# One decoder layer on one core: another order in the attention cycles, the output product from rounded parts, and weight rests on GpSimd

## The chip, the cores and the metric
One core of a Trainium2 chip. The metric is device time in microseconds (us), one execution of the whole kernel; the median of several runs is given. Engines are named PE (TensorE), DVE (VectorE), ACT (ScalarE), POOL (GpSimd) and SP (SyncE, which issues most DMAs).

## The reference
The input is x, 8 sequences of 128 rows of 512 features, with a context of the same size. Three blocks follow each other, each with a residual sum and a LayerNorm after it. Cut to what matters:

```python
# block 1: polynomial unit and gated unit, both on x
approx = (x @ up_w.T) @ local_out.T + sum over 6 orders (d**m/m! * (x @ up_w.T)) @ fuse[m].T
block1 = approx + (silu(x @ g1.T) * (x @ u1.T)) @ d1.T
# block 2: cross attention, 32 heads of 128, no score scaling
q, k, v = rmsnorm(x) @ w_q.T, ctx @ w_k.T, ctx @ w_v.T
score = q @ k.T + position_bias        # -inf where the mask is False
block2 = x + (softmax(score) @ v) @ w_out.T
# block 3: gated unit with weights of -1, 0 and 1
block3 = ((silu((x @ Wg.T) * ag) * ((x @ Wu.T) * au)) @ Wd.T) * ad
```

The mask lets a row attend only to keys in the last 32 positions of a sequence.

## The kernel before
Batch elements go in two halves of four (512 tokens each). PE multiplies float32 data in two ways. An exact product takes plain float32 operands. A product "from rounded parts" splits both operands into a part rounded to fp32r on ACT (`*_hi`) and the rest `whole - hi` on DVE (`low`, L1288, `*_lo`), and adds hi*hi, hi*lo and lo*hi (`passes`, L543).

The attention stage is `attention(few)`. A mask with keys only in the last FEW = 32 positions takes the branch `few=True`, and that one runs here. It walks n from -7 to 64 over HN = 64 pairs of head and half. `shared(n)` is true for n 0 to 15 and 32 to 47: such a cycle makes keys and values of a head for both halves at once (256 columns, from rounded parts) and keeps the other half's piece (`kept_k`, `kept_v`). In n 16 to 31 and 48 to 63, which the code calls `late`, the kept pieces are used, and `keys` and `values` only raise their semaphores. Keys run LEAD_K = 7 ahead, queries LEAD_T = 6 ahead.

What PE does in a sharing cycle n is written out by hand, in this order: `queries(n+6)` into bank 0, `turn(n-1)` (transpose of the probabilities, bank 3), `weigh(n-2)` (output product, one tile of 32 rows per batch element, into the four acc banks), `keys(n+7)` (bank 1), `values(n)` (bank 3), `outer(n-1)` (values times output weights, bank 1), and in two cycles of four a half of `group_scores` (bank 2). In a late cycle: queries, keys if n+7 is sharing, turn, weigh, outer, values, scores. ACT copies every bank out to SBUF, in an order of its own: in a sharing cycle `copy_queries`, `copy_turned`, `split_k(n+8)`, `copy_keys`, `split_v(n+1)`, `copy_values`, `copy_outer`, `exponentials(n+1)`. DVE does `find_max`, `divide`, `add_mask`, `rest_k` and `rest_v`. Each engine works in the order of its program.

These waits stand around the change. `outer(n-1)` waits for the copy of `keys(n+7)`, since both use bank 1:

```python
pe.wait_ge(v_ok, n + 1)
pe.wait_ge(k_ok, min(n + LEAD_K + 2, HN))
pe.wait_ge(kept_k_ok, shared_count(min(n + LEAD_K + 1, HN - 1)))
```

`copy_keys` and `copy_values` of a sharing cycle are two ACT instructions each: the kept 128x128 piece (L1150, L1183), then 128x512 (L1153, L1186). The last block starts after the loop: `features` transposes its input into bank 0 in n = 62 and 63, `gate` and `up` of its first tile follow at n = 64.

POOL normalises rows (L480, L485) and takes a maximum over partitions (L509); it has nothing to do in most of the attention stage.

## Time and profile before

| | us |
|---|---|
| median of 3 runs | 755.46 (755.07 to 755.62) |
| the profiled execution | 753.72 |
| its span in the trace | 751.9 |
| PE busy | 716.2 |
| DVE busy | 522.2 |
| ACT busy | 408.6 |
| POOL busy | 94.8 |

The kernel has three stages in the trace: block 1 up to about 222 us, attention up to about 613 us, the last block to the end. A PE instruction's record is longer than the distance to the next one, because matmuls overlap; what a step costs PE is the distance from its first start to the next step's first start.

### The profile page before, as it was taken

Reading aid. Unit: us, or ns where it says so; the run is one execution under the profiler, and the core shown is the slowest. Engines: PE = TensorE matmul, PEld = TensorE weight load, DVE = VectorE, ACT = ScalarE, POOL = GpSimd, SP = SyncE. Lnnn points to the kernel's source line nnn. Section 1 sums busy time; section 2 is a strip of 40 time slices with the busy share of each in tenths; the row PEclk is TensorE's granted clock in tenths of the full one; section 3 lists DMA queues with packets and bytes.
Section 4 is the critical chain, followed back from the end, with each engine's and each line's share of the span. In section 5 each row is a group of like instructions: output and inputs, shape, how many; then the busy total and the mean of one; then the engine's idle time right before and its main releaser. Section 6 shows DMA issues by size and latency. Waiting matters only on the chain.

```text
span 751.9 us, 12237 instructions
## 1 busy us (share of the span) xinstructions
PE 716.2 (95%) x4082; PEld 555.7 (74%) x4082; DVE 522.2 (69%) x848; ACT 408.6 (54%) x747; POOL 94.8 (13%) x88
## 2 busy tenths in 40 slices
PE   8999999999999999999999999999999779998993
PEld 6788888888878878776667787877656257886882
DVE  6555687588664875686876678667897828669565
ACT  6333323432355676776776666666676644454552
POOL 2000000074003600000000000000050004105403
PEclk9999999999999999999999999999999999999997
DMA  8455532545556765677997776668785513442631
GB/s 307 152 206 206 179 119 70 163 168 187 183 208 199 251 195 181 216 258 233 306 316 236 240 238 190 192 215 267 263 297 180 169 44 117 135 151 98 204 122 56
DMA packets 70681, 145.10 MB, mean 193 GB/s; under 512 B 7920, under 2 KB 8192, under 8 KB 69984
## 3 DMA queue, kind: packets, MB, share of 16 engines
q1 hardware_dynamic: 69200, 137.26, 55.7%
q0 software_dynamic: 1200, 6.70, 2.3%
q8 instruction: 34, 0.56, 0.3%
q10 hardware_dynamic: 224, 0.39, 0.2%
q14 instruction: 23, 0.19, 0.1%
HBM read 142.23 MB, written 2.10 MB: 192 GB/s over the span
## 4 chain that ended last, share of the span: by engine, by line
PE 86%; DVE 5%; issue 3%; DMA 2%; ACT 2%; POOL 1%; SPq 0%; ACTq 0%; DVEq 0%; POOLq 0%
PE bank L543 38%; PE acc L543 16%; PE acc L846 8%; PE bank L751 7%; PE bank L824 7%; PE bank L716 7%; PE bank L778 1%; PE bank L729 1%; DMA b_raw<-b 1%; DMA a_raw<-a 1%; PE bank L575 1%; DVE tile_lo L1288 1%; ACT v_sb L1186 1%; DVE a_lo L1288 1%; DMA wq<-wqn 1%
## 5 line engine op out<-in xcount | busy, mean ns | idle before, releaser
L543 PE MATMUL bank<-feat_hi,a_hi 128*128 128x512 f32 x348 | 137.7, 396 | 2.2 <-ACT u_sb L1193 0.8
L543 PE MATMUL bank<-feat_lo,a_hi 128*128 128x512 f32 x348 | 136.5, 392 | 2.1 <-issue 2.1
L1288 DVE TENSOR_TENSOR a_lo<-a_raw,a_hi 128x1024 fp32r<-128x1024 f32 (+3 forms) x47 | 56.8, 1208 | 94.5 <-ACT a_hi L1000 86.9
L543 PE MATMUL acc<-b_hi,tile_hi 128*128 128x512 f32 x224 | 87.8, 392 | 4.9 <-DVE tile_lo L1288 3.0
L543 PE MATMUL acc<-b_hi,tile_lo 128*128 128x512 f32 x224 | 87.3, 390 | 0.0
L543 PEld LDWEIGHTS bank<-feat_hi,a_hi 128*128 128x128 f32 x348 | 65.9, 189 | 22.6 <-issue 4.0
L543 PEld LDWEIGHTS bank<-feat_lo,a_hi 128*128 128x128 f32 x348 | 65.9, 189 | 13.5
L846 PE MATMUL acc<-u_sb,prob_t 32*128 32x512 f32 x512 | 73.0, 640 | 0.0
L543 PE MATMUL bank<-feat_hi,a_lo 128*128 128x512 f32 x180 | 70.1, 389 | 0.0
L1017 ACT ACTIVATE tile_hi<-pair 128x512 fp32r<-128x512 f32 x54 | 33.9, 628 | 66.3 <-DVE pair L1350 37.4
L751 PEld LDWEIGHTS bank<-t_ring,xn 128*128 128x128 f32 x512 | 62.1, 192 | 8.5 <-issue 7.2
L445 POOL TENSOR_SCALAR scale<-moments 128x4 f32<-128x4 f32 (+1 forms) x9 | 2.6, 287 | 515.1 <-DVEq L1420 514.8
L1558 DVE TENSOR_REDUCE row_sum<-prob 128x4 f32<-128x512 f32 x64 | 43.7, 683 | 31.9 <-ACT prob L1174 30.5
L1160 ACT ACTIVATE t_ring<-bank 128x512 f32<-128x512 f32 x64 | 38.2, 597 | 46.3 <-PE bank L716 46.0
L751 PE MATMUL bank<-t_ring,xn 128*128 128x128 f32 x512 | 62.3, 275 | 0.0
L1193 ACT ACTIVATE u_sb<-bank 128x512 f32<-128x512 f32 x64 | 38.2, 598 | 28.4 <-PE bank L824 25.8
L543 PEld LDWEIGHTS acc<-b_hi,tile_hi 128*128 128x128 f32 x224 | 42.0, 188 | 15.6 <-DVE b_lo L1288 4.2
L543 PE MATMUL acc<-b_lo,tile_hi 128*128 128x512 f32 x136 | 52.9, 389 | 0.0
L1288 DVE TENSOR_TENSOR b_lo<-b_raw,b_hi 128x512 fp32r<-128x512 f32 x56 | 40.0, 715 | 14.9 <-ACT b_hi L1007 14.6
L1007 ACT ACTIVATE b_hi<-b_raw 128x512 fp32r<-128x512 f32 x56 | 34.8, 623 | 26.8 <-PE acc L543 21.6
L1026 ACT ACTIVATE gated<-bank 128x512 f32<-128x512 f32 x20 | 12.0, 598 | 67.8 <-PE bank L543 67.8
L543 PEld LDWEIGHTS acc<-b_hi,tile_lo 128*128 128x128 f32 x224 | 42.1, 188 | 8.6
(152 smaller groups left out, 1555.8 us busy)
## 6 DMA issues: line engine op xcount, KB each, us to landing
wqi<-ax SPq DMA_DIRECT2D x64, 256.0 KB, 3.3
wq<-wqn SPq DMA_DIRECT2D x64, 256.0 KB, 3.7
wv<-wvh SPq DMA_DIRECT2D x64, 256.0 KB, 4.0
wo<-bx SPq DMA_DIRECT2D x64, 256.0 KB, 4.0
a_raw<-w SPq DMA_DIRECT2D x22, 512.0 KB, 4.1
wk<-ax SPq DMA_DIRECT2D x43, 256.0 KB, 3.8
a_raw<-a SPq DMA_DIRECT2D x21, 512.0 KB, 5.4
b_raw<-b SPq DMA_DIRECT2D x34, 256.0 KB, 2.7
```

The lines of the kernel that those rows point to most:

```text
L543: mm = pe.matmul(out_ap, w, x, start=start and k == 0, stop=stop and k == len(products) - 1, skip_group_check=True)
L716: mm = pe.matmul(bank[0][:, c * P:(c + 1) * P], wq[par][:, c * P:(c + 1) * P], few_keys, start=True, stop=True)
L751: mm = pe.matmul(bank[2][:, b * P:(b + 1) * P].rearrange("p (k h) -> p h k", h=GH), xn[half][:, c, b * SEQ:(b + 1) * SEQ], t_ring[g % 2][: ...
L824: mm = pe.matmul(bank[1][:], few_values, wo[slot][:], start=True, stop=True)
L846: mm = pe.matmul(acc[b][:], prob_t[par][rows, 0:P], u_sb[par][rows, :], start=begins, stop=ends, skip_group_check=True)
L1007: act.activation(b_hi[par][:], b_raw[par][:], ACT.Copy).then_inc(b_hi_ok, 1)
L1017: act.activation(tile_hi[par][:], src, ACT.Copy).then_inc(tile_hi_ok, 1)
L1026: act.activation(gated[:], bank[0][:], ACT.Silu).then_inc(silu_ok, 1)
L1160: act.activation(t_ring[n // GH % 2][:, n % GH].rearrange("p c b k -> p (c b k)"), bank[0][:], ACT.Copy).then_inc(t_ok, 1)
L1193: act.activation(u_sb[n % 2][:], bank[1][:], ACT.Copy).then_inc(u_ok, 1)
L1288: return dve.tensor_tensor(out_ap, whole, high, ALU.subtract)
L1558: dve.tensor_reduce(row_sum[:], prob[n % 2][:], AX_X, ALU.add).then_inc(sum_ok, 1)
```

## The change
In sharing cycles PE's order becomes queries, `values(n)`, `weigh(n-2)`, `turn(n-1)`, `keys(n+7)`, `outer(n-1)`, scores. `turn(n-1)` now waits for the copy of `values(n)`, which has bank 3 before it. `weigh` of a sharing head becomes 12 matmuls of fp32r parts in place of 4 float32 ones: the rounded parts `p_hi` and `u_hi` come from ACT, the rests `p_lo` (128x128) and `u_lo` (128x512) from DVE. The rests of the key and value weights go from DVE to POOL, but for the first nine keys and two values. ACT's order in a sharing cycle becomes copy_queries, copy_values, copy_turned with p_hi, split_v(n+1), split_k(n+8), copy_keys, copy_outer, exponentials.

In late cycles `values` (semaphores only) comes right after `turn` without its wait for the copy of the turned probabilities, and ACT does `copy_values` before `copy_outer`. The features of the last block move to n = 58 and 59, the first gate to n = 61, the first up to n = 62 and into bank 2, and SP loads the next tiles at n = 58. New buffers are fitted in for these.

```diff
@@ PE, the attention loop
+                    if n == FEATURES_2 + 1:
+                        features(2, 3, resid[:, TT:2 * TT, :], HN)
+                    if 0 <= n < HN and not late:
+                        values(n)
+                        if n >= 2:
+                            weigh(n - 2)
                     if n >= 1:
                         turn(n - 1)
-                    if 2 <= n < HN:
+                    if few and late:
+                        values(n)
+                    if late:
                         weigh(n - 2)
...
                     if n >= 0 and not late and n + LEAD_K < HN:
                         keys(n + LEAD_K)
...
                     if late:
                         outer(n - 1)
-                    if 0 <= n < HN:
-                        values(n)
...
                     if n >= 1 and not late:
                         outer(n - 1)
+                    if n == GATE_30:
+                        pe.wait_ge(feat_lo_ok, C)
+                        gate(A30, A30 % 2, 0, HALVES * F1, last=True)
+                    if few and n == UP_30:
+                        pe.wait_ge(added_ok, HN)
+                        up(A30 % 2, 0, HALVES * F1, last=True, into=bank[2])
@@ turn(n)
+                    made = n + 1 if n + 1 < HN and shared(n + 1) else n
                     pe.wait_ge(prob_ok, n + 1)
-                    pe.wait_ge(v_ok, n + 1)
-                    pe.wait_ge(kept_v_ok, shared_count(n))
+                    pe.wait_ge(v_ok, made + 1)
+                    pe.wait_ge(kept_v_ok, shared_count(made))
@@ weigh(n)
+                    if few and shared(n):
+                        for k, (weights, values_) in enumerate(((p_hi, u_hi), (p_hi, u_lo), (p_lo, u_hi))):
+                            for b in range(HB):
...
+                                mm = pe.matmul(acc[b][:], weights[par][rows, :], values_[par][rows, :], start=begins and k == 0,
+                                               stop=ends and k == 2, skip_group_check=True)
@@ ACT, the attention loop
+                if n >= 0 and not late:
+                    copy_values(n)
                 if n >= 1:
                     copy_turned(n - 1)
+                if n >= -1 and n + 1 < HN and shared(n + 1):
+                    split_v(n + 1)
                 if n > 0 and n + LEAD_K + 1 < HN and shared(n + LEAD_K + 1):
                     split_k(n + LEAD_K + 1)
...
                 if n >= 0 and not late and n + LEAD_K < HN:
                     copy_keys(n + LEAD_K)
-                if n + 1 == 0 or n >= 0 and shared(n) and shared(n + 1):
-                    split_v(n + 1)
                 if late:
+                    copy_values(n)
                     copy_outer(n - 1)
-                if n >= 0:
-                    copy_values(n)
@@ POOL, after the maximum over partitions
+            for n in range(POOL_V - 1, HN):
+                if n + 1 < HN and shared(n + 1):
+                    pool.wait_ge(wv_hi_ok, shared_count(n + 1))
+                    pool.tensor_tensor(wv_lo[(n + 1) % 2], wv[(n + 1) % 2][:], wv_hi[(n + 1) % 2].bitcast(F32),
+                                       ALU.subtract).then_inc(wv_rest_ok, 1)
+                k = n + LEAD_K + 1
+                if k < HN and shared(k):
+                    pool.wait_ge(wk_hi_ok, shared_count(k))
+                    pool.tensor_tensor(wk_lo[k % 2], wk[k % WK_RING][:], wk_hi[k % 2].bitcast(F32),
+                                       ALU.subtract).then_inc(wk_rest_ok, 1)
@@ DVE
+            def rest_p(n):
+
+                dve.wait_ge(p_hi_ok, shared_count(n))
+                dve.wait_ge(turned_ok, n + 1)
+                low(p_lo[n % 2][:], prob_t[n % 2][:, 0:P], p_hi[n % 2][:].bitcast(F32)).then_inc(p_lo_ok, 1)
+
+            def rest_u(n):
+
+                dve.wait_ge(u_ok, n + 1)
+                low(u_lo[n % 2][:], bank[1][:], u_hi[n % 2][:].bitcast(F32)).then_inc(u_lo_ok, 1)
```

## Rows read from the trace of the kernel before

**Rows 1.** The page: busy time by engine, and the chain that ended last.
```profile
PE 716.2 (95%) x4082; PEld 555.7 (74%) x4082; DVE 522.2 (69%) x848; ACT 408.6 (54%) x747; POOL 94.8 (13%) x88
PE 86%; DVE 5%; issue 3%; DMA 2%; ACT 2%; POOL 1%; SPq 0%; ACTq 0%; DVEq 0%; POOLq 0%
```
**Rows 2.** Windows: stretch, length, busy of PE, PEld, DVE, ACT, POOL, clock, DMA.
```profile
257.00:347.00 90.00, 89.46 (x656) 70.01 (x654) 60.69 (x103) 61.31 (x128) 0.66 (x3) 1.00 0.64 206
```
**Rows 3.** Timeline, PE, a sharing cycle: start, length, instruction.
```profile
277.79 1.02 PE L824 MATMUL bank<-wo,v_sb 128*128 128x512 f32 x2
278.65 1.05 PE L716 MATMUL bank<-k_ring,wq 128*128 128x128 f32 x8
279.54 0.28 PE L778 MATMUL bank<-ident_r,prob 128*128 128x128 f32 x1
279.74 1.14 PE L846 MATMUL acc<-u_sb,prob_t 32*128 32x512 f32 x8
...
283.78 1.02 PE L824 MATMUL bank<-wo,v_sb 128*128 128x512 f32 x2
```
**Rows 4.** The chain that ended last: keys and values together; a down product of block 1.
```profile
44.63 2.72 PE acc L543 x12
...
280.88 3.06 PE bank L543 x24
```
**Rows 5.** Timeline, same cycle: the last matmul of keys and the ACT work behind.
```profile
282.22 0.28 PE L543 MATMUL bank<-a_hi,wk_lo 128*128 128x256 f32 x1
...
282.54 0.28 ACT L1150 ACTIVATE b_raw<-bank 128x128 f32<-128x128 f32 x1 [1.09 <-PE bank L543]
...
282.72 0.59 ACT L1153 ACTIVATE k_ring<-bank 128x512 f32<-128x512 f32 x1
...
283.19 0.63 ACT L1069 ACTIVATE b_hi<-wv 128x512 fp32r<-128x512 f32 x1
```
**Rows 6.** Timeline, PE: weigh in two sharing cycles without keys.
```profile
327.70 1.14 PE L846 MATMUL acc<-u_sb,prob_t 32*128 32x512 f32 x8
...
332.46 1.14 PE L846 MATMUL acc<-u_sb,prob_t 32*128 32x512 f32 x8
```
**Rows 7.** Timeline, a late cycle: outer, queries, turn, outer on PE.
```profile
365.98 1.12 PE L824 MATMUL bank<-wo,kept_v 128*128 128x512 f32 x2
366.95 1.05 PE L716 MATMUL bank<-b_raw,wq 128*128 128x128 f32 x8
...
368.33 0.36 PE L778 MATMUL bank<-ident_r,prob 128*128 128x128 f32 x1 [0.33 <-ACT v_sb L1186]
...
369.69 1.12 PE L824 MATMUL bank<-wo,kept_v 128*128 128x512 f32 x2
```
**Rows 8.** Timeline, ACT: the copy of values that the turn of rows 7 waits for.
```profile
367.64 0.59 ACT L1186 ACTIVATE v_sb<-bank 128x512 f32<-128x512 f32 x1
```
**Rows 9.** Groups by form, POOL: a sum of two 128x512 tiles.
```profile
L518 POOL TENSOR_TENSOR resid<-normed,resid 128x512 f32<-128x512 f32 x7 | 10.1, 1473 | 75.0 <-DVE normed L1401 38.7 <-DVE normed L1654 36.3
```
**Rows 10.** Timeline, PE, DVE and POOL at the start of the attention.
```profile
248.05 0.36 PE L543 MATMUL bank<-a_hi,wk_hi 128*128 128x256 f32 x1
...
248.79 0.68 DVE L1288 TENSOR_TENSOR b_lo<-wv,b_hi 128x512 fp32r<-128x512 f32 x1
...
250.20 3.57 POOL L485 TENSOR_SCALAR normed<-resid,rms_scale 128x512 f32<-128x512 f32 x2
...
251.63 0.69 DVE L1562 TENSOR_TENSOR prob<-prob,row_inv 128x512 f32<-128x512 f32 x1
...
263.12 0.38 POOL L509 PARTITION_ALL_REDUCE piece_all<-piece_all  x1 [6.03 <-issue]
```
**Rows 11.** Timeline, PE: the end of the attention.
```profile
578.45 0.28 PE L778 MATMUL bank<-ident_r,prob 128*128 128x128 f32 x1
...
613.14 0.47 PE L543 MATMUL bank<-feat_hi,a_hi 128*128 128x512 f32 x1 [0.67 <-issue]
```

More of the change, by code:

```diff
@@ L127, in sem @@
             return ctx.enter_context(nc.semaphore(name))
+        with ExitStack() as sharing:
+            u_lo = [sharing.enter_context(nc.sbuf_tensor(f"u_lo{i}", [P, D], F32R)) for i in range(2)]
         a_raw, a_hi, a_lo = two("a_raw", [P, 2 * C * P]), two("a_hi", [P, 2, C, P], F32R), two("a_lo", [P, 2, C, P], F32R)
@@ L154, in decoder_kernel @@
         wk.append(gated)
+        with ExitStack() as sharing:
+            u_hi = [sharing.enter_context(nc.sbuf_tensor(f"u_hi{i}", [P, D], F32R)) for i in range(2)]
         u_sb = two("u_sb", [P, D])
@@ L177, in decoder_kernel @@
         piece = [raw.bitcast(I32) for raw in piece_raw]
+        with ExitStack() as sharing:
+            p_hi = [sharing.enter_context(nc.sbuf_tensor(f"p_hi{i}", [P, P], F32R)) for i in range(2)]
         mask_words = sb("mask_words", [P, BATCH, SEQ // 4], U32)
@@ L180, in decoder_kernel @@
         mask_add = [sb(f"mask_add{j}", [P, BATCH, P], BF16) for j in range(GH)]
+        with ExitStack() as sharing:
+            p_lo = [sharing.enter_context(nc.sbuf_tensor(f"p_lo{i}", [P, P], F32R)) for i in range(2)]
         few_add, key_scale = sb("few_add", [P, BATCH, FEW]), sb("key_scale", [P, 2])
@@ L846, in weigh @@
                             mm = pe.matmul(acc[b][:], prob_t[par][rows, 0:P], u_sb[par][rows, :], start=begins, stop=ends,
+                                           skip_group_check=True)
+                        elif shared(n):
+                            columns = slice(b * P, (b + 1) * P)
+                            pe.matmul(acc[b][:], u_hi[par][:, columns].bitcast(F32), wo[slot][:], start=begins, stop=False,
+                                      skip_group_check=True)
+                            mm = pe.matmul(acc[b][:], u_lo[par][:, columns].bitcast(F32), wo[slot][:], start=False, stop=ends,
                                            skip_group_check=True)
@@ L877, in attention @@
                     late = 0 <= n < HN and not shared(n)
+                    if not few and 0 <= n < HN and j < 2:
+                        for m in range(n + 1, n + 2 + j):
+                            head_scores(m)
                     if late and n + LEAD_K < HN:
@@ L954, in last_block @@
                 transposes(3, 1, bank[3], x1)
-                gate(a, a % 2, 0, s0 + f, low=low)
+                gate(a, a % 2, 0, s0 + f, low=low, last=True)
                 pe.wait_ge(feat_lo_ok, C + 1)
@@ L1166, in copy_turned @@
                     act.wait_ge(out_used, n - 1)
+                if shared(n):
+                    act.activation(p_hi[n % 2][:], bank[3][:, 0:P], ACT.Copy).then_inc(p_hi_ok, 1)
                 act.activation(prob_t[n % 2][:], bank[3][:], ACT.Copy).then_inc(turned_ok, 1)
@@ L1349, in product @@
                 if last_block:
[L1350 removed]
+                    dve.scalar_tensor_tensor(out=hidden[mpar], in0=second[:], scalar=const[:, bass.ds(f + COL_AU, 1)],
                                              in1=gated[:], op0=ALU.mult, op1=ALU.mult).then_inc(hidden_ok, 1)
@@ L1571, in _ @@
                 m = n + 1
-                if n == 2 * BLOCK:
-                    rest_v(n)
+                if n >= 2 and shared(n - 2):
+                    rest_u(n - 2)
                 if 0 <= m < HN and m % GH > 0:
                     find_max(m)
+                if n == FEATURES_2:
+                    chunk(2, 0, bank[0])
+                if n == FEATURES_2 + 1:
+                    chunk(2, 3, bank[0])
                 if n >= 0:
@@ L1582, in _ @@
                     rest_k(n + LEAD_K + 2)
-                elif n > 0 and n + LEAD_K + 1 < HN and shared(n + LEAD_K + 1):
-                    rest_k(n + LEAD_K + 1)
+                if n >= 1 and shared(n - 1):
+                    rest_p(n - 1)
+                if 0 <= m < POOL_V:
+                    rest_v(m)
                 if 0 <= m < HN:
```

151 lines of the change are left out of this document (95 added, 56 removed).

## The prediction
> **What bounds the kernel now.** I read the page first. PE is busy for 95% of the span and holds 86% of the chain that ended last [rows 1]. So time is won or lost by what PE does and by what it waits for. The windows say how tight the attention is: in the 90 us of the first sharing block PE is busy for 89.46 us, while DVE and ACT have 60.69 and 61.31 and POOL 0.66 [rows 2]. POOL and DVE have room; PE has none.
>
> The PE timeline of one sharing cycle gives its price list. Each step costs the distance to the next first start: outer 278.65 - 277.79 = 0.86, queries 0.89, turn 0.20, then weigh from 279.74 to the first matmul of keys at 280.88 = 1.14, and keys and values together to the next outer at 283.78 = 2.90, so 1.45 each. The cycle is 283.78 - 277.79 = 5.99 us [rows 3, 4]. There is no gap in it, and the reader should see why: the two banks that hold keys and values (1 and 3) are written in turns with other steps between. ACT copies keys out of bank 1 while PE makes values in bank 3, and only then does outer write bank 1.
>
> **The price of a copy that nothing covers.** The last matmul of keys starts at 282.22 and its slot is a twelfth of 1.45, so it ends at 282.34. ACT starts at 282.54, 0.20 later. The kept piece goes first, the large copy starts 0.18 after it at 282.72 and takes 0.59 [rows 5]. PE starts 0.10 after such a copy ends: 367.64 + 0.59 = 368.23, turn at 368.33 [rows 7, 8]. Sum: 0.20 + 0.18 + 0.59 + 0.10 = 1.07 us from the end of the products to the next user of the bank. Behind a 128x512 copy the next ACT instruction starts after 0.47; a split is 0.63 long where a copy is 0.59, so I take 0.52 behind it [rows 5].
>
> **The new sharing cycle with keys (n up to 8, and 32 to 40).** The order puts two steps on one bank next to each other twice.
> - values, then turn, both in bank 3. Only weigh lies between. Old weigh costs 1.14. The new one has 12 matmuls in three rounds of four 32-row tiles. If four tiles run side by side as the float32 ones do, a round costs about one fp32r matmul, 2.72/12 = 0.227 [rows 4], so weigh is near 0.7 to 0.9. Turn can start only 1.07 after values. The gain of the rounded parts, 0.2 to 0.4 per cycle, is therefore hidden behind the copy: what I book is 1.14 - 1.07 = 0.07.
> - keys, then outer, both in bank 1, with nothing between. At best the gap is 1.07. ACT is in program order, and before `copy_keys` it now has p_hi, prob_t, split_v and split_k, which begin 0.20 after turn: 0.18 + 0.47 + 0.52 + 0.52 = 1.69, so `copy_keys` starts 1.89 after turn, where the end of keys alone would allow 1.45 + 0.20 = 1.65. Gap: 1.07 + 0.24 = 1.31.
>
> Cycle: queries 0.89 + values 1.45 + copy 1.07 + turn 0.20 + keys 1.45 + gap 1.31 + outer 0.86 = 7.23, which is 1.24 more than 5.99. Cycles with scores add the same 1.8 to 2.3 before and after, since the scores stand behind outer in both. For n = 1 to 7 and 32 to 39 that is 15 x 1.24 = 18.6. n = 40 has no split_k: +1.0. n = 8 has feature transposes in the gap: +0.2.
>
> **The new sharing cycle without keys (n = 9 to 15, 41 to 47).** `keys` is only a semaphore there, but ACT still copies bank 1, and outer still waits for it. Now this copy stands behind p_hi, prob_t and split_v, which come after turn: 0.20 + 0.18 + 0.47 + 0.52 + 0.59 + 0.10 = 2.06 from the end of turn to outer. Cycle: 0.89 + 1.45 + 1.07 + 0.20 + 2.06 + 0.86 = 6.53. Before, such a cycle took 332.46 - 327.70 = 4.76 [rows 6]. Twelve cycles x 1.77 = 21.2. The last of each block (15, 47) has no split_v, 0.52 less, so 1.25 each: 2.5.
>
> **Start.** Three things come once, with n = 0 to 2. `values(0)` now stands before `keys(7)`, and its rest is made at 248.79 + 0.68 = 249.47 on DVE [rows 10], where PE started keys at 248.05: +1.5 with the wait for the rest's arrival. Cycle 1 has no weigh to cover the copy: +1.1. And POOL reaches its new loop only after the maximum over partitions, which ends at 263.5 [rows 10]. `values(2)` needs POOL's first rest, 1.47 for a 128x512 tile with two SBUF inputs [rows 9], so at about 265.1; PE, already late, would be there at about 262.8: +2.3. Together 4.9.
>
> **Rests on DVE and POOL.** DVE loses two instructions of 0.69 and gains `rest_u` of the same size and a small `rest_p`; with six instructions of 0.69, a reciprocal and `rest_p` it has some 4.7 us of work in a cycle of 6.5 or 7.2: nothing on the path. `rest_u(n-2)` holds bank 1 until about 1.6 us into the cycle, keys come at 3.6. POOL has two rests, about 3 us. Its rest for values(n+1) can start when split_v ends, about 5.1 us into cycle n, and is there at 6.6; PE asks at 7.4 in the shorter cycle. Price 0 while POOL stays under 2.2 us each.
>
> Here a rule speaks against the change. In the trace, DVE subtracts (0.68) and multiplies (0.69, at 251.63) in usual time while POOL works on SBUF tiles around it from 250.20 [rows 10]. The Trainium skill, "SBUF — State Buffer", section "Who interferes with whom", says that a DVE instruction with two SBUF inputs and a GpSimd instruction that reads SBUF exclude each other for the whole instruction. By that rule each POOL rest could wait for a DVE one. The trace shows no such wait on DVE's side; it stays as the POOL rival below.
>
> **Late cycles.** The stall of turn on the copy of v goes, since `copy_values` now precedes `copy_outer`. A cycle without scores took 369.69 - 365.98 = 3.71 [rows 7]; its steps are outer 366.95 - 365.98 = 0.97 [rows 7], queries 0.89 and turn 0.20 [rows 3], and weigh about 1.07 (behind weigh a step starts about 0.1 late: in rows 3 that is in weigh's 1.14, here in outer's 0.97 for 0.86) = 3.13. ACT has five copies and an exponential in it, 5 x 0.47 + 0.52 = 2.87, so 3.13 just fits. About nine such cycles x 0.58 = 5.2. Cycles with scores had no stall. In the 14 or so late cycles that also carry keys or splits there is 0.1 each: 1.3. `weigh(15)` and `weigh(47)` wait about 0.5 for `rest_u`, which gives 1.0 back to the loss. Net gain 5.5, bounds 3 and 7.
>
> **The end.** From turn(57) at 578.45 to the last block's code at 613.14 are 34.7 us [rows 11]. The change moves gate, up and features into the gaps of the last heads, where PE waits for DVE. But the four feature rests (0.69 each, each a round from PE over ACT to DVE and back of about 2.1) now stand before the masks of the last four heads, in DVE's order too, so that chain starts about 5.8 us later and then needs its five instructions of 0.69 and a reciprocal, 3.7 per head. Followed step by step this gives 35.2, against 34.7. I take +0.5, bounds -3 and +4.
>
> **Sum.** 18.6 + 1.0 + 0.2 + 21.2 + 2.5 + 4.9 - 5.5 + 0.5 = 43.4. On the profiled execution, 753.72 + 43.4 = 797.1. The median of the runs stands 1.74 above that execution, so 798.9. I say 798.5.
>
> **Rivals.**
> 1. *ACT does not hold the copies back* (only the bare 1.07 gap counts, split_v and split_k slip in elsewhere). Takes 15 x 0.24 + 12 x 0.52 = 9.8 off, and with a milder start about 14: 784. For it: ACT is busy two thirds of the time. Against it: its order is fixed.
> 2. *POOL becomes the bound in sharing cycles.* If a rest takes 2.2 or waits 0.7 for DVE, values wait up to 0.8 in the 12 short cycles: +10, 809. For it: the margin is 0.8.
> 3. *The 32-row tiles don't overlap in fp32r.* Then weigh is 12 x 0.227 = 2.72 in place of 1.07 under the copy: 30 x 1.65 = 50 more, 848. No row shows fp32r with 32 rows; the eight float32 records in 1.14 us [rows 3] speak against it.
> 4. *Faster: the bank waits don't bind.* If outer after keys and turn after values started without a gap, the cycle would keep its sum of steps, weigh would save 0.3 x 30 = 9, and the late cycles 5.5 more: 741. It decides if the exposed gap is below 0.3 us; the 1.07 of [rows 5, 7] stands against it, and so does the stall of 0.33 that turn shows already [rows 7].
> 5. *It doesn't do what it says* (the time stays within 0.2%). The gains and losses would have to cancel; nothing points there.
>
> **Chances.** Forecast 0.67, rival 1 0.12, rival 2 0.11, rival 3 0.05, rival 4 0.04, rival 5 0.01. The forecast's own terms give 789 to 806 (ends of late cycles, end, start). The range takes in rivals 1 and 2: 781 to 811, and leaves out 3 to 5 and the tails. About 0.2%, 1.5 us, is what a measurement of this kernel can tell from no change. Faster by more than that 0.04, within it 0.01, slower 0.95.
>
> **What would show it.** In the trace of after, ACT v_sb should stand as the releaser of turn in sharing cycles, and ACT k_ring as the releaser of outer, each before an idle time: the sharing cycle without scores should be 7.2 us with keys and 6.5 without, and PE busy in the first block well below 99%. Weigh should be 0.7 to 0.9 us. POOL should show 53 subtractions of about 1.5 us and no one waiting for them but `values(2)`. Late cycles without scores should be 3.1 to 3.3. The prediction is wrong if outer starts less than 0.5 us after keys, if late cycles gain more than 1 us each, or if the last heads run without waits.

## The result, and the profile after

| | before | after |
|---|---|---|
| median of the runs shown | 755.27 us | 833.83 us |
| profiled execution | 753.72 us | 835.31 us |
| its span, mean granted clock | 751.9 us, 0.992 | 833.5 us, 0.962 |

The ratio is 1.1044, with a 95% interval of 1.1023 to 1.1065. The kernel lost 78.6 us where the forecast had 43.4. The direction was right, the size was not. Each ratio below is against the kernel before as measured beside that run (medians 754.78 to 755.88 us), so differences between two runs of the section below are good to about 1 us. The page of after, busy time and the chain that ended last, beside [rows 1]:

```profile
PE 742.5 (89%) x4210; PEld 580.8 (70%) x4210; DVE 519.4 (62%) x859; ACT 417.2 (50%) x779; POOL 163.0 (20%) x141
PE 72%; ACT 8%; DVE 7%; issue 6%; POOL 4%; DMA 2%; SPq 0%; ACTq 0%; DVEq 0%; POOLq 0%
```

PE held 86% of the chain and now holds 72%: ACT, DVE and POOL have come into it. The windows say where (columns as in [rows 2]): the same 90 us of the first sharing block; the last cycles without keys of that block (the late ones begin at 391.59); PE's stall at the start of the attention and what came behind it.

```profile
257.00:347.00 90.00, 70.58 (x515) 56.82 (x515) 39.00 (x73) 47.01 (x104) 22.25 (x20) 0.94 0.43 146
...
347.00:392.00 45.00, 35.99 (x228) 27.88 (x227) 22.63 (x41) 20.79 (x45) 5.07 (x4) 0.84 0.45 152
264.00:272.00 8.00, 0.00 (x0) 0.00 (x0) 0.67 (x1) 0.24 (x1) 0.70 (x2) 0.74 0.18 66
272.00:278.00 6.00, 5.23 (x28) 4.29 (x29) 0.00 (x0) 1.05 (x4) 1.87 (x2) 0.50 0.01 3
```

PE is busy for 70.58 of 90 us where it was 89.46; 9.16 of the missing time is the one stall at the start. And there is something that the forecast does not have at all: the granted clock is 0.94 and 0.84 in these stretches, and 0.50 from 272 to 278.

One sharing cycle with keys, PE (start, length, instruction, idle time before it and its releaser); the twelve matmuls each of values (from 298.34) and keys (from 301.26) are left out. It answers to [rows 3]:

```profile
296.60 1.10 PE L874 MATMUL bank<-wo,v_sb 128*128 128x512 f32 x2 [0.94 <-ACT k_ring L1240]
297.53 1.05 PE L758 MATMUL bank<-k_ring,wq 128*128 128x128 f32 x8
...
299.94 0.50 PE L901 MATMUL acc<-u_hi,p_hi 32*128 32x512 f32 x4
300.28 0.41 PE L901 MATMUL acc<-u_lo,p_hi 32*128 32x512 f32 x4
300.51 0.41 PE L901 MATMUL acc<-u_hi,p_lo 32*128 32x512 f32 x4
300.91 0.36 PE L821 MATMUL bank<-ident_r,prob 128*128 128x128 f32 x1
...
303.87 1.10 PE L874 MATMUL bank<-wo,v_sb 128*128 128x512 f32 x2 [0.94 <-ACT k_ring L1240]
```

ACT in the same cycle:

```profile
300.22 0.59 ACT L1275 ACTIVATE v_sb<-bank 128x512 f32<-128x512 f32 x1
301.31 0.28 ACT L1255 ACTIVATE p_hi<-bank 128x128 fp32r<-128x128 f32 x1 [0.49 <-PE bank L821]
301.48 0.59 ACT L1256 ACTIVATE prob_t<-bank 128x512 f32<-128x512 f32 x1
301.96 0.64 ACT L1156 ACTIVATE b_hi<-wv 128x512 fp32r<-128x512 f32 x1
302.48 0.63 ACT L1147 ACTIVATE wk_hi<-wk 128x512 fp32r<-128x512 f32 x1
303.00 0.28 ACT L1237 ACTIVATE b_raw<-bank 128x128 f32<-128x128 f32 x1
303.16 0.61 ACT L1240 ACTIVATE k_ring<-bank 128x512 f32<-128x512 f32 x1
```

The copy of the values ends at 300.22 + 0.59 = 300.81 and turn starts at 300.91. Then ACT has p_hi, prob_t, two splits and the kept piece before the copy of keys, which ends at 303.77, and outer starts at 303.87. The cycle is 303.87 - 296.60 = 7.27 us, against a forecast of 7.23 and 5.99 before. Outer shows its wait for k_ring. Turn shows none, because the record of the third round of weigh runs to 300.92: that it is the copy which holds it is read from the two times, 300.81 and 300.91.

Where the time went, from the starts of `queries` in the two traces (differences of the same head; 753.72 + 81.6 = 835.3):

| stretch | after - before, us | forecast |
|---|---|---|
| cycles n = 0 and 1 | 3.7 | 1.5 + 1.1 + 1.2 |
| n = 2, above what a sharing cycle loses | 11.4 | 2.3 |
| 16 cycles with keys (2 to 8, 32 to 40) | 19.3 | 18.6 |
| 14 cycles without keys (9 to 15, 41 to 47), at full clock | 25.9 | 23.7 |
| the same, what the half clock adds | 14.3 | 0 |
| late cycles, with the first two behind each sharing block | 4.4 | -5.5 |
| from n = 57 to the end | 2.7 | 0.5 |

"At full clock" is read from the run `e3_filler` below: 54.5 + 53.9 us for these fourteen cycles, against 41.6 + 40.9 before and 60.8 + 61.9 after. The 14.3 is that of the profiled execution. It varies: the same fourteen cycles lost 7.6 in the trace of `e1_max_late`, where nothing in them was changed. The terms in which the order was costed held within 10%. The stall in n = 2, the clock and the late cycles did not. The end took 2.2 us more than its forecast, within the bounds of -3 and +4.

### The profile page after: what moved, and what is told of

Its sections match the earlier page's. It is cut to its first block, busy times and chain, and to the rows that moved or that the text cites. A ratio compares the mean times of both kernels' runs of the same rounds, so it can differ in the third digit from the quotient of the medians.

```text
span 833.5 us, 12717 instructions
## 1 busy us (share of the span) xinstructions
PE 742.5 (89%) x4210; PEld 580.8 (70%) x4210; DVE 519.4 (62%) x859; ACT 417.2 (50%) x779; POOL 163.0 (20%) x141
## 4 chain that ended last, share of the span: by engine, by line
PE 72%; ACT 8%; DVE 7%; issue 6%; POOL 4%; DMA 2%; SPq 0%; ACTq 0%; DVEq 0%; POOLq 0%
PE bank L580 30%; PE acc L580 14%; PE bank L874 7%; PE bank L793 6%; PE bank L758 5%; PE acc L901 3%; PE acc L912 3%; ACT b_hi L1156 2%; PE bank L821 2%; ACT k_ring L1240 2%; POOL resid L506 1%; ACT prob_t L1256 1%; ACT wk_hi L1147 1%; PE bank L771 1%; DMA b_raw<-b 1%
## 5 line engine op out<-in xcount | busy, mean ns | idle before, releaser
L580 PE MATMUL bank<-feat_hi,a_hi 128*128 128x512 f32 x260 | 101.8, 392 | 0.4 <-DVE a_lo L1383 0.2
L580 PE MATMUL bank<-feat_lo,a_hi 128*128 128x512 f32 x260 | 101.2, 389 | 0.0
L542 POOL TENSOR_TENSOR b_lo<-wv,b_hi 128x512 fp32r<-128x512 f32 x30 | 38.3, 1276 | 190.4 <-ACT b_hi L1156 183.1
L793 PEld LDWEIGHTS bank<-t_ring,xn 128*128 128x128 f32 x512 | 68.1, 207 | 10.1 <-issue 8.4
L874 PE MATMUL bank<-wo,v_sb 128*128 128x512 f32 x64 | 41.1, 728 | 38.1 <-ACT k_ring L1240 38.0
L1383 DVE TENSOR_TENSOR u_lo<-bank,u_hi 128x512 fp32r<-128x512 f32 x32 | 22.1, 691 | 78.5 <-ACT u_hi L1282 78.5
L1247 ACT ACTIVATE t_ring<-bank 128x512 f32<-128x512 f32 x64 | 38.2, 596 | 59.4 <-PE bank L758 59.1
L580 PEld LDWEIGHTS bank<-feat_hi,a_hi 128*128 128x128 f32 x260 | 48.8, 188 | 11.8 <-DVE a_lo L1383 1.9
L580 PEld LDWEIGHTS bank<-feat_lo,a_hi 128*128 128x128 f32 x260 | 48.8, 188 | 10.0
L580 PE MATMUL acc<-b_lo,tile_hi 128*128 128x512 f32 x136 | 52.9, 389 | 0.0
L580 PE MATMUL bank<-a_hi,b_hi 128*128 128x256 f32 x128 | 40.1, 313 | 10.1 <-POOL b_lo L542 9.3
L1658 DVE TENSOR_TENSOR score<-score,neg_max 128x512 f32<-128x512 f32 x64 | 47.2, 737 | 2.2
```

The costliest lines, as they stand in the source:

```text
L542: pool.tensor_tensor(wv_lo[(n + 1) % 2], wv[(n + 1) % 2][:], wv_hi[(n + 1) % 2].bitcast(F32), ALU.subtract).then_inc(wv_rest_ok, 1)
L580: mm = pe.matmul(out_ap, w, x, start=start and k == 0, stop=stop and k == len(products) - 1, skip_group_check=True)
L793: mm = pe.matmul(bank[2][:, b * P:(b + 1) * P].rearrange("p (k h) -> p h k", h=GH), xn[half][:, c, b * SEQ:(b + 1) * SEQ], t_ring[g % 2][: ...
L874: mm = pe.matmul(bank[1][:], few_values, wo[slot][:], start=True, stop=True)
L1247: act.activation(t_ring[n // GH % 2][:, n % GH].rearrange("p c b k -> p (c b k)"), bank[0][:], ACT.Copy).then_inc(t_ok, 1)
L1383: return dve.tensor_tensor(out_ap, whole, high, ALU.subtract)
```

## The experiments

### The start: the maximum over partitions in front of POOL's loop

POOL in after, start of the attention:

```profile
263.45 0.38 POOL L535 PARTITION_ALL_REDUCE piece_all<-piece_all  x1 [6.01 <-issue]
263.89 0.19 POOL L537 CAST low_flag<-piece_all 128x1 int32<-128x1 f32 x1
...
271.38 1.25 POOL L542 TENSOR_TENSOR b_lo<-wv,b_hi 128x512 fp32r<-128x512 f32 x1 [7.30 <-issue]
```

and PE, the first matmul of values(2):

```profile
272.77 0.55 PE L580 MATMUL bank<-a_hi,b_hi 128*128 128x256 f32 x1 [9.16 <-POOL b_lo L542]
```

In before, [rows 10] had shown 6.03 us of idle time ahead of the all-reduce; the forecast took it as lateness of POOL and let the first subtraction follow at once. But 7.30 us more stand behind it, in which POOL waits for nothing that the profile shows. The edit moves it:

```diff
-            pool.wait_ge(top_ok, 1)
-            pool.partition_all_reduce(piece_all[:, 1:2], ...)
...
             for n in range(POOL_V - 1, HN):
...
+            pool.wait_ge(top_ok, 1)
+            pool.partition_all_reduce(piece_all[:, 1:2], ...)
             normalise(2)
```

> The changed kernel with one thing moved: POOL makes the maximum over partitions (the all-reduce and the small cast behind it, 263.45 to 264.08 in the trace of the changed kernel) only behind its loop of rests. Everything else stays. Theory: POOL stands 7.30 us idle between that cast and its first subtraction because of what stands before it, not because of the subtraction's inputs; without it the first subtraction starts when split_v is done, PE's wait of 9.16 us before values(2) shrinks to under 1, and the granted clock does not fall behind it. 7.3 to 9.2 us and about 2 of the half clock: 823 to 825 against 833.8. Rival: the first subtraction of a loop on POOL costs that time itself (first use of that instruction, or its inputs come late): then the idle time stays before the first subtraction, and the time stays within 1 us of 833.8.

Measured: 819.55 us, ratio 1.085 (1.0821 to 1.088); 14.3 less than after. That is more than the 9 to 11 expected. The two traces are 18.4 apart: 11.4 of that is cycle 2, and 6.6 are cycles without keys that kept the full clock more often here, though nothing in them was changed. How often they do so differs between executions. POOL, same place:

```profile
257.65 1.27 POOL L537 TENSOR_TENSOR b_lo<-wv,b_hi 128x512 fp32r<-128x512 f32 x1 [0.75 <-ACT b_hi L1156]
```

The first subtraction now waits for its split only, cycle 2 takes 9.05 us for 20.44, and the rival is out: it was not the subtraction that was slow to start, but what stood before it. The idle time ahead of the all-reduce moved with it (5.75 us at 587.06, where nobody waits). The cast behind the all-reduce starts at once in both kernels, so the 7.30 us belong to the change from these two to the subtraction; which of the two is to blame is not separated. The Trainium skill says in "GPSIMD Engine Reference", section "2.1 Instruction dispatch", that POOL's kernels can be loaded at run time and that the first call to a freshly loaded one costs about 6 us which no instruction in the profile shows. The 5.75 to 6.03 us ahead of the all-reduce are of that size and the 7.30 behind it are more; that a load is what happens there is not shown by any run.

### Whose rests: POOL or DVE

> The changed kernel with all rests of the key and value weights on DVE again (behind the small rest of the probabilities, value weights first, then key weights), none on POOL. Theory: POOL's rests cost only at the start (7 to 9 us of PE's idle time there, and the half clock behind it) and 0.2 to 0.4 us in some late cycles that carry keys; in the steady sharing cycles of 7.27 and 6.58 us they are hidden, and DVE, which has about 4.7 us of work in them, takes 0.69 or 1.38 more without becoming the bound. So 822 to 826. Rival: DVE becomes the bound in the cycles with keys (4.7 + 1.38 = 6.1 of 7.27, with its waits more than that), and the cycles grow to 7.5 or more: 826 to 832. Second rival: POOL's rests do hold the steady cycles back; then the cycle with keys falls below 7.2 here.

The edit takes POOL's loop out; `rest_v` and `rest_k` follow `rest_p` on DVE, and PE waits for `wk_lo_ok` and `wv_lo_ok` throughout. Measured: 819.77 us, ratio 1.084 (1.0804 to 1.0876), below the expected 822 to 826 and the same as e1_max_late. The cycles with keys stay at 7.27 (n = 3: 7.27, after 7.28). So POOL's rests do not hold the steady cycle, and DVE can carry them too. Late cycles that carry keys gain: n = 28 takes 4.80 for 5.04, n = 29 7.05 for 7.28, n = 32 7.23 for 7.63.

The kernel before with nothing but the rests on POOL (the maximum behind them):

> The kernel before (754.8 us) with nothing but the rests of key and value weights on POOL in place of DVE (the maximum over partitions behind them, so that it costs nothing at the start). Theory: a subtraction takes 1.27 to 1.35 us on POOL for 0.69 on DVE, and where a DVE instruction with two inputs in SBUF meets it, that one takes up to 1.8 for 0.69; DVE has a third of its time free in these cycles, so PE, which is busy 99% of them, waits for none of it but in the late cycles that carry keys (0.24 to 0.34 in two of them): 754.5 to 756.5. Rival: the collisions reach PE through prob or the masks in several cycles: 757 to 762. Second rival: DVE relieved of 1.4 us per cycle hands prob over earlier somewhere: below 753.

Measured: 757.76 us, ratio 1.0026 (1.0013 to 1.0039), 2.2 more, a little over the range of the theory and at the lower end of the rival. In the trace the sharing cycles are as before to 0.01 us. Three late cycles are longer, n = 25 by 0.56, n = 28 by 0.33, n = 29 by 0.34, and `keys` waits that much more (0.76 us at 390.09, for 0.22 before): what reaches PE is the rest, which is longer on POOL. In n = 25 it is stretched as well, 1.45 us for 1.27, behind a DVE multiplication that had begun 0.37 us before it:

```profile
388.43 1.45 POOL L514 TENSOR_TENSOR wk_lo<-gated,wk_hi 128x512 fp32r<-128x512 f32 x1 [45.62 <-ACT wk_hi L1079]
```

These 1.2 us are in the trace; the other one of the 2.2 I can't place. The gain of 1.4 us of DVE time per cycle buys nothing, since nobody waited for DVE. What it costs where nobody waits is seen in two rows of that run, DVE and POOL:

```profile
334.88 1.78 DVE L1571 TENSOR_TENSOR score<-score,neg_max 128x512 f32<-128x512 f32 x1
```

```profile
334.83 1.28 POOL L518 TENSOR_TENSOR b_lo<-wv,b_hi 128x512 fp32r<-128x512 f32 x1 [3.56 <-ACT b_hi L1088]
```

A DVE sum of two SBUF operands, 0.69 elsewhere, takes 1.78: it starts 0.05 behind POOL's subtraction and ends 0.55 behind POOL's end. Twelve DVE instructions of this run are stretched so between 257 and 500 us. In [rows 10], beside POOL's scalar instructions, the same kind of DVE instruction kept its 0.69, and the forecast left the rule open. The Trainium skill, "SBUF — State Buffer", section "Who interferes with whom", says that such a pair exclude each other, and that the one issued first goes through. Here the trace agrees, for two TENSOR_TENSORs; for the scalar instructions of [rows 10] it does not, though they read SBUF too.

In after it happens only three times in the attention (at 450.94, 455.92 and 474.20 us, 1.61 to 1.68 for 0.69), since POOL's rests fall where DVE reads a bank or idles. That is luck of the order, and it ends when the order changes (section "The order").

### The clock: filling the gap

After, PE without the small matmuls, in a cycle without keys that lost time:

```profile
343.61 0.36 PE L821 MATMUL bank<-ident_r,prob 128*128 128x128 f32 x1
345.87 1.55 PE L874 MATMUL bank<-wo,v_sb 128*128 128x512 f32 x2 [1.91 <-ACT k_ring L1240]
347.21 3.18 PE L793 MATMUL bank<-t_ring,xn 128*128 128x128 f32 x16
```

Outer waits 1.91 us for ACT, as costed (2.06 from the end of turn). But then outer takes 1.55 for 1.10 and the scores 3.18 for 1.95, and the windows show why:

```profile
341.00:345.00 4.00, 2.96 (x28) 2.19 (x26) 1.42 (x4) 2.37 (x6) 0.00 (x0) 1.00 0.39 135
346.00:349.00 3.00, 3.00 (x11) 2.24 (x12) 0.91 (x2) 1.12 (x2) 0.62 (x1) 0.56 0.49 179
```

The granted clock is 0.56: PE is at the lower of its two levels, 1.2 for 2.4 GHz, for most of that stretch. Eleven of the fourteen cycles without keys have a gap of 1.91 us, and nine of these eleven lose 1.4 to 1.7 us in this way. At full clock such a cycle is 6.58 us (360.82 to 367.40, weigh to weigh; forecast 6.53). To see whether PE's idle time is the cause, work that nobody needs was put into the gap, on top of e1_max_late:

```diff
+                    if few and n >= 10 and not late and n + LEAD_K < HN and not shared(n + LEAD_K):
+                        pe.wait_ge(t_ok, n + LEAD_T + 1)
+                        for _ in range(14):
+                            pe.matmul(bank[0][:, 0:HALVES * P], few_hi[:, 0, 0:P], few_hi[:, 0, :], start=True, stop=True,
+                                      skip_group_check=True)
```

> The kernel of e1_max_late (819.5 us) with idle work added: in the sharing cycles without keys (heads 10 to 15 and 41 to 47), between turn and outer, PE makes 14 more products of 128x128 with 128x256 (0.12 us each, 1.7 us in all) of an operand that is there anyway, into the bank of the queries, which ACT has copied by then; nobody reads them. They fill the 1.9 us in which outer waits for ACT's copy. Theory: the granted clock falls to half in these cycles because PE idles in them; with the gap filled it stays at full speed, and the cycles of 7.0 to 10.0 us go back to what they are at full clock (6.58, with scores 8.3 to 8.8): 13 cycles, in all 8 us less, 811 to 813, though PE does 22 us more of matmuls. Rival: the clock falls for another reason: then it is 819.5 or, where the fillers run at half clock past the gap, 825 or more.

Measured: 811.14 us, ratio 1.0742 (1.0715 to 1.0768): 8.4 less than e1_max_late with 182 more matmuls. PE in the same cycle, n = 10, and a window over it:

```profile
332.15 0.36 PE L822 MATMUL bank<-ident_r,prob 128*128 128x128 f32 x1
332.50 1.91 PE L979 MATMUL bank<-a_hi 128*128 128x256 f32 x14
334.42 1.10 PE L875 MATMUL bank<-wo,v_sb 128*128 128x512 f32 x2
335.35 1.95 PE L794 MATMUL bank<-t_ring,xn 128*128 128x128 f32 x16
```

```profile
332.00:337.00 5.00, 4.99 (x36) 4.07 (x33) 1.11 (x3) 2.94 (x7) 1.27 (x1) 1.00 0.55 193
```

The gap is full, the clock 1.00, outer back at 1.10 and the scores at 1.95, and the cycle takes 8.36 us where after has 10.01 and e1_max_late 9.62. In n = 14 it is 8.36 for 10.03. PE's idle time is what takes its clock away, and this costs on top of the idle time itself.

### The order

The order of before put back, on top of e1_max_late, with everything else of the change kept (on POOL the key rest first):

```diff
-                    if 0 <= n < HN and not late:
-                        values(n)
-                        if n >= 2:
-                            weigh(n - 2)
                     if n >= 1:
                         turn(n - 1)
+                    if n >= 2 and n < HN and not late:
+                        weigh(n - 2)
...
+                    if 0 <= n < HN and not late:
+                        values(n)
```

> The kernel of e1_max_late (819.5 us) with the order of the kernel before in the sharing cycles, on PE, ACT and POOL (turn, weigh, keys, values, outer); the rounded output product, its rests on DVE, the rests on POOL, and the changes to late cycles and end stay. Theory: the order is what costs the 1.27 and 1.84 us per cycle, as each bank is used twice in a row. What is left is the rest of u: weigh and keys wait until DVE has read bank 1, 1.68 us behind outer (0.20 + 0.59 + 0.10 + 0.69 + 0.10), where queries and turn cover 1.09; with weigh at 0.7 the cycle with keys is 6.1 to 6.2 us (before 5.99, changed kernel 7.27) and the one without keys 4.7 to 4.8 (before 4.76, changed 6.58), and the half-clock stretches go. 15 x 1.1 + 12 x 1.85 + 8 for the clock + 3 at the start = 50 less: 766 to 773. Rival: POOL's rests, DVE's two more instructions or the rounded product cost time of their own: then the cycles stay at 6.6 or more and the time above 785.

Measured: 766.61 us, ratio 1.0162 (1.0145 to 1.0179): 52.9 less than e1_max_late. The opposite, the kernel before with the new order alone:

> The kernel before (754.8 us) with nothing but the new order in the sharing cycles (values, weigh, turn, keys, outer on PE, and ACT's copies and splits to match); float32 output product, all rests on DVE, late cycles and end as before. Theory: the order is the whole loss in the cycles, and the other parts hardly touch it. Cycles with keys 7.2 to 7.3 us (copy of the values over the float32 product of 1.14 covers itself, then 0.9 before outer), cycles without keys 6.4 to 6.6 at full clock, 3 us at the start, and 8 to 12 us of half clock: 754.8 + 15 x 1.25 + 12 x 1.75 + 3 + 10 = 805 to 811. Rival: a good part of the loss came from the copies and rests that the rounded product adds on ACT and DVE: then the cycles are under 7.0 and 6.2, and the time under 798.

Measured: 806.75 us, ratio 1.0679 (1.0654 to 1.0705), so 51.2 more. Its cycles with keys are 7.22 to 7.31, those without 6.54 at full clock. Both say the same from two sides: of the 78.6 us, the order is some 51 to 53, half-clock stretches included. The rival that the extra copies and rests had a large share is out. With the 14.3 of e1_max_late that leaves the 11.8 us by which e5_old_order is above the kernel before (754.78 beside it): the product, the rests, the late cycles and the end together.

e5_old_order also shows what the rounded product needs. DVE's rest of u, and PE from there to the second outer:

```profile
272.69 0.69 DVE L1380 TENSOR_TENSOR u_lo<-bank,u_hi 128x512 fp32r<-128x512 f32 x1 [1.45 <-ACT u_hi L1277]
272.75 0.28 PE L821 MATMUL bank<-ident_r,prob 128*128 128x128 f32 x1
273.59 0.51 PE L896 MATMUL acc<-u_hi,p_hi 32*128 32x512 f32 x4 [0.56 <-issue]
...
277.46 1.02 PE L869 MATMUL bank<-wo,v_sb 128*128 128x512 f32 x2
...
283.92 1.02 PE L869 MATMUL bank<-wo,v_sb 128*128 128x512 f32 x2
```

Weigh stands 0.56 idle behind turn. The profile names no releaser, but weigh waits for the rest of u, which DVE finishes at 273.38. Cycles with this wait take 6.46 (outer to outer, 283.92 - 277.46), others 5.84; the mean of the seven without scores is 6.1, in the range of the theory, and no better than the 5.99 of before. Seventeen DVE instructions are stretched beside POOL here, among them a multiplication of 1.22 for 0.69 at 282.00.

### The output product

e4_float_weigh takes the rounded product, its copy p_hi, its two rests and their waits out, and keeps the order:

> The changed kernel with the output product of the sharing cycles in float32 again (one product of four row tiles, about 1.1 us, in place of three rounded ones, about 0.7), without the rounded copy of the probabilities, without the two rests of it and of u on DVE, and without the waits on them; the order and POOL's rests stay. Theory: the shorter product is wholly hidden behind ACT's copy of the values (1.07 us from values to turn), so it gains nothing, and its rests and waits cost little: the cycle with keys goes from 7.27 to between 7.1 and 7.3, the one without keys from 6.58 to between 6.4 and 6.6 at full clock (0.18 less before the copy of the probabilities), the two cycles behind each sharing block lose their wait for the rest of u (about 1 us each). PE is 0.4 us busier in each cycle, so the half-clock stretches may become fewer: 822 to 832. Rival: the rounded product was worth its 0.4 us in each of 30 cycles: then 844 or more.

Measured: 826.17 us, ratio 1.0911 (1.0868 to 1.0955), 7.7 less than after. The cycle with keys goes from 7.27 to 7.23 only; the product was hidden, as costed. The four cycles behind the sharing blocks gain 4.0 of the 7.7: n = 16 takes 3.52 for 4.30 and n = 17 5.78 for 7.02, where in after PE stands still for DVE:

```profile
398.41 0.36 PE L821 MATMUL bank<-ident_r,prob 128*128 128x128 f32 x1 [1.46 <-DVE u_lo L1383]
```

This `turn` does not need u. The skipped `keys` ahead of it, which is only a semaphore there, waits for the rest of u before it raises it.

### The late cycles

The same skipped `keys` waits for ACT's copy of u in all late cycles. Without that wait (kept in the two cycles behind each sharing block):

```diff
-                    if n > LEAD_K + 1:
+                    if n > LEAD_K + 1 and (shared(n) or shared(n - LEAD_K - 2) or not few):
                         pe.wait_ge(u_ok, n - LEAD_K - 1)
```

> The changed kernel without one wait: in the late cycles, where keys is only a semaphore, PE waits there for ACT's copy of u before it goes on to turn; here it does not (save in the two cycles behind each sharing block, where DVE still reads that bank). Theory: this wait is what took the place of the stall of turn on the copy of the values: without it turn fills the 0.4 to 0.5 us between the end of the copy of u and its own start, and the late cycle without scores falls from 3.63 to 3.1 to 3.3 us; 14 or so such cycles with a wait: 828 to 831. Rival: weigh, right behind turn, waits for the same copy, and ACT with its 2.9 us of work is the bound: then the cycle stays above 3.5 and the time within 1.5 us of 833.8.

Measured: 830.55 us, ratio 1.1002 (1.0961 to 1.1042), 3.3 less; the interval touches that of after. The time lies in the expected range. The late cycles without scores do what the theory says, and yet the block does not: n = 20 and n = 24 fall from 3.63 and 3.62 to 3.14 and 3.13, the forecast's number. But n = 18 to 31 take 71.4 us as in after (71.3). PE in e6_late_wait, the two waits that take the gain back:

```profile
414.90 1.14 PE L912 MATMUL acc<-u_sb,prob_t 32*128 32x512 f32 x8 [1.49 <-DMA wv<-wvh]
...
432.25 0.36 PE L580 MATMUL bank<-a_hi,wk_hi 128*128 128x256 f32 x1 [0.84 <-POOL wk_lo L547]
```

The first is a wait in the skipped `values` for weights that a late head does not use (0.28 in after); the second is POOL's rest, 0.44 in after. So the wait for that load was moved off PE too, to the queue that loads the next ones (SP), now on the kernel before and with the new late order alone:

```diff
                 if n >= 2:
                     sp.wait_ge(v_mm, n - 1)
+                    if not shared(n - 2):
+                        sp.wait_ge(wv_dma[n % 2], 16 * (n // 2))
...
+                    if few and not shared(n):
+                        pe.sem_inc(v_mm, 1)
+                        return
                     pe.wait_ge(wv_dma[par], 16 * (n // 2 + 1))
```

> The kernel before (755.9 us) with only the late cycles changed: ACT copies the values before u, PE no longer waits for u in a keys step that is only a semaphore, and the wait for the value weights that a late head doesn't use is moved from PE to the queue that loads the next ones. Theory: the late cycle after two score cycles goes from 3.71 to 3.14 us; there are seven such cycles in 32, and in the first late block the load of weights sets the pace behind them, so that part of it is given back: 752.5 to 755. Rival: all late cycles gain 0.5 to 0.6, as I had forecast: 748 to 750.

Measured: 750.09 us, ratio 0.9933 (0.9912 to 0.9954). It beats both kernels, by 4.7 and 83.7 us. PE, a late cycle of it (answers to [rows 7]):

```profile
366.64 1.05 PE L718 MATMUL bank<-b_raw,wq 128*128 128x128 f32 x8
367.53 0.28 PE L780 MATMUL bank<-ident_r,prob 128*128 128x128 f32 x1
367.74 1.14 PE L848 MATMUL acc<-u_sb,prob_t 32*128 32x512 f32 x8
368.81 1.13 PE L826 MATMUL bank<-wo,kept_v 128*128 128x512 f32 x2
369.77 1.05 PE L718 MATMUL bank<-b_raw,wq 128*128 128x128 f32 x8
```

No wait is left, and the cycle is 3.13. n = 16 to 32 take 83.95 us for 86.33, n = 49 to 56 35.08 for 36.36. Only n = 20, 24 and 56 took 3.70 or 3.71 in before; n = 19, 23, 51 and 55 were at 3.13 already. My theory had too little (752.5 to 755), its rival (all late cycles) too much at 748 to 750; the result lies between, at the rival's edge.

### The end

The kernel before with the new end alone:

> The kernel before (754.8 us) with nothing but the new end: the features of the last block made within heads 58 and 59, gate and up within heads 61 and 62, their loads earlier (and the split of the value weights of head 32 one cycle earlier). The order of the sharing cycles, the product in float32, the rests on DVE and the late cycles are as before. Theory: this is what the forecast put at +0.5 (-3 to +4): the feature rests stand before the masks of the last heads on DVE, head 58 takes 8.1 us for 4.0, and what is made early does not pay for it: +1.5 to +3, 756 to 758. Rival: the early gate and up are a gain that the changed kernel hid behind other losses: 751 to 753.

Measured: 759.94 us, ratio 1.0057 (1.0044 to 1.007): 4.4 more, above the range and the forecast's upper bound of +4. PE behind the last weigh, which starts at 613.44:

```profile
618.60 0.76 PE L570 MATMUL bank<-last_hi,a_hi 128*128 128x512 f32 x1 [4.02 <-issue]
621.82 0.79 PE L570 MATMUL bank<-last_lo,a_hi 128*128 128x512 f32 x1 [1.61 <-issue]
```

4.02 + 1.61 = 5.63 us of idle time at the entry to the last block, which waits for nothing that the profile shows, where before had 0.67 [rows 11] and 2.13 (at 616.20). It is 3.26 in after (at 696.06). In the traces t1_end_only is 6.0 us longer from n = 57 on: 1.9 up to the last weigh, 4.1 behind it, and the entry is 2.8 of these. Why it takes 2.8 in one kernel and 5.6 in another, no run here tells.

### A version that should have beaten both

b2_lagged is b1_late_only, which has the old order, with the rounded product, POOL's rests (the maximum behind them), an order of loads near that of after, and in cycles with keys `weigh(n - 3)` ahead of `turn(n - 1)`:

```diff
+    if few and shared(n) and n + LEAD_K < HN and shared(n + LEAD_K):
+        return [m for m in (n - 3, n - 2) if m >= 0 and shared(m) == (m == n - 3)], []
...
+                    for m in due(n, few)[0]:
+                        weigh(m)
                     if n >= 1:
                         turn(n - 1)
```

> A version that should beat both. It is b1_late_only with the rounded output product, its rests on DVE, and the rests of key and value weights on POOL, in the order of the kernel before, with two differences: the maximum over partitions comes behind POOL's loop, and in cycles with keys the output product is that of one head earlier (three cycles behind, in place of two) and stands before turn, so that queries, weigh and turn (0.89 + 0.7 + 0.2 = 1.79) cover the 1.68 us until DVE has made the rest of u from bank 1. Theory: no bank is then used twice in a row without cover, and the shorter product (0.7 for 1.14) is a gain of 0.4 in each of 17 cycles with keys (5.55 to 5.65 us for 5.99); cycles without keys stay at 4.7 to 4.8: 745 to 750. Rival: DVE, ACT or POOL can't keep up with 5.6 us (ACT has 4.7, DVE 4.7 in it): then the cycle with keys stays at 5.9 or more, and the time at 754 or above.

Measured: 755.57 us, ratio 1.0014 (0.9998 to 1.003): no gain over before, and 5.5 worse than b1_late_only. PE, a cycle with keys:

```profile
272.63 0.51 PE L894 MATMUL acc<-u_hi,p_hi 32*128 32x512 f32 x4
272.97 0.40 PE L894 MATMUL acc<-u_lo,p_hi 32*128 32x512 f32 x4
273.20 0.39 PE L894 MATMUL acc<-u_hi,p_lo 32*128 32x512 f32 x4
273.53 0.39 PE L818 MATMUL bank<-ident_r,prob 128*128 128x128 f32 x1
```

Nothing waits here, and the product takes 273.53 - 272.63 = 0.90 from its start to the next step, for 1.14 in float32. The cycle is 5.83 for 5.99: the rounded product in its new place, with nothing to hide it, is worth 0.16 us. I had expected 0.4, from the rounds' own 0.7. In other cycles more than that is lost: n = 5 takes 8.94 for 8.24. DVE's two rows ahead of it, and PE's `keys` in it, which waits for the rest of u (278.46 is its weigh):

```profile
275.33 1.82 DVE L1644 TENSOR_TENSOR prob<-prob,row_inv 128x512 f32<-128x512 f32 x1
277.08 1.35 DVE L1359 TENSOR_TENSOR p_lo<-prob_t,p_hi 128x128 fp32r<-128x128 f32 x1
```

```profile
280.37 0.36 PE L579 MATMUL bank<-a_hi,wk_hi 128*128 128x256 f32 x1 [0.62 <-DVE u_lo L1359]
```

Both DVE instructions (0.69 and 0.28 elsewhere) lie beside POOL's rests (275.31 to 276.60 and 276.74 to 278.28) and take 2.2 us more than elsewhere. DVE starts the rest of u at 279.55, 1.28 us behind the end of ACT's copy of u, where one cycle earlier it was 0.03 us. That is the stretching of p1_pool_only again, and this time it reaches PE.

## Why the prediction was wrong, point by point

- **What bounds the kernel, and the price of an uncovered copy**: right. The bare copy was put at 1.07, and turn starts 1.06 behind the end of values (299.73 + 0.12 to 300.91), 0.10 behind the copy as read from [rows 7, 8].
- **New cycle with keys**: 7.23 forecast, 7.27 measured. ACT k_ring is the releaser of outer, as named. The sign for turn, ACT v_sb before an idle time, came only once (0.90 us at 256.41, n = 1): weigh takes 0.97 from start to start, above the 0.7 to 0.9 forecast, and its record hides what is left of the wait. Weigh is hidden (e4_float_weigh).
- **New cycle without keys**: 6.53 forecast, 6.58 at full clock. The step that failed is the one that was not there: the working treated PE's clock as given. The stretches of half clock cost 14.3 us in fourteen cycles of the profiled execution. This is the largest part of the miss, and e3_filler shows its cause; by medians, filling the gap gave 8.4.
- **Start**: "`values(2)` needs POOL's first rest, ... so at about 265.1; +2.3". This step failed: 7.30 us of idle time stand between the all-reduce's cast and the first subtraction, PE waited 9.16, and ran at a clock of 0.50 behind it. 11.4 in the trace, 14.3 in the runs of e1_max_late.
- **Rests on DVE and POOL**: priced at 0. In after this holds for sharing cycles (mostly 1.25 to 1.30 us a rest for the 1.47 taken). For late cycles with keys it is 0.2 to 0.4 each in n = 28, 29 and 32, which I had not looked at; alone the move costs 2.2 us.
- **Late cycles**: -5.5 forecast, +4.4 measured. Two faults. The step "about nine such cycles x 0.58" counted cycles that were not there (in before three of n = 16 to 56 have the 3.71, see b1_late_only), took away the stall on the copy of v, and did not ask what is late next: the skipped `keys` waits for the copy of u, 0.5 us later than turn could go, and behind it stand the loads. And "`weigh(15)` and `weigh(47)` wait about 0.5" was sized for the wrong instruction: the wait is in the skipped `keys`, up to 1.46 in one cycle, and the four cycles take 3.7 us more.
- **End**: +0.5 forecast, +2.7 in the trace and +4.4 alone. Alone, 2.8 are the entry to the last block, which nothing in the trace of before announces. In after the entry costs only 0.5 more than before (3.26 for 2.80), and the other 2.2 were not taken apart.
- **Rivals**: 1 (784) and 4 (741) are out, since the copies do hold outer and turn. 3 is out: three rounds start 0.34 and 0.23 apart. 2 had POOL as a bound in the steady cycles; POOL was one, but at the start. 5 (no change) is out. The range, 781 to 811, was made of rivals 1 and 2 and had no case for a cost of idle time that is more than the idle time.

Sum of the miss, from the table: clock 14.3, start 9.0, late cycles 9.9, cycles at full clock 2.9, end 2.2; together 38.3, for 81.6 - 43.4 = 38.2.

## What to carry to other kernels

Before steps on one bank are moved next to each other, price the copy between them on the other engine's program order: a timeline of one cycle gives that to 0.05 us. Then ask two more questions: does the engine now idle in every cycle, so that its clock falls, and does a step that is only a semaphore still wait for something? An instruction that only gives an idle engine something to do (1.4 us of DVE time here) gains nothing, and a product that is shorter by 0.44 on paper gave 0.16.

## What the runs showed of the hardware

- PE ran at 1.2 GHz in place of 2.4 for part of nine of the eleven cycles with a gap of 1.91 us (granted clock 0.56 from 346 to 349 us in after). 14 useless matmuls in the gap of thirteen cycles made the kernel 8.4 us faster.
- POOL stood 7.30 us idle behind PARTITION_ALL_REDUCE and its cast before its first TENSOR_TENSOR, and 6.01 ahead of the all-reduce (5.75 to 6.03 in the kernels looked at).
- A DVE instruction with two SBUF inputs takes up to 1.85 us for 0.69 beside a POOL TENSOR_TENSOR, and is not stretched beside POOL's TENSOR_SCALAR of [rows 10] (0.69 at 251.63). A POOL TENSOR_TENSOR that began behind such a DVE instruction took 1.45 for 1.27.
- Four tiles of 32 rows in fp32r overlap: 12 matmuls of 512 columns in 0.90 us from the first start to the next step (b2_lagged).
- At the entry to the last block's code PE idled for 2.80 us in before, 3.26 in after and 5.63 in t1_end_only, with nothing in the profile that it waited for.
